# Half of each tile's gathered rows turned by VectorE in 32 by 32 blocks, and the place matmul on 128 rows

## The chip, the cores and the metric

The kernel runs on one core of one Trainium2 chip. The metric is the device time of one execution in microseconds (us). Each time of the kernel before is a median over three executions, or one profiled execution where that is said.

## The reference

448 tokens (64 sequences of 7 patches) go through three layers, one after the other. A patch of 16 by 64 values is layer-normed, multiplied by a 1024 x 512 matrix and layer-normed again. A feed-forward layer with ternary weights and 8-bit activations (1408 wide, SwiGLU) is added. Then a mixture of 32 experts with 8 chosen per token is added. The change lies in that last layer, so this is the part to keep in mind:

```
logits = x @ router_w.T ; probs = softmax(logits)
rw, sel = top_k(probs, 8) ; rw = rw / sum(rw)
for each expert e of 32:
    w_e = sum(where(sel == e, rw, 0))
    h = silu(x @ wg) * (x @ wu)          # 512 -> 192, twice
    acc = acc + (h @ wd) * w_e           # 192 -> 512
```

All of this is float32. An expert is chosen by 112 tokens on average (448 x 8 / 32), by some more, by some less.

## The kernel before

The kernel is written by hand, engine by engine, with semaphores. The first third of the program computes the two dense layers and the router. What follows is a loop over 32 **tiles**. Tile t holds the first 128 tokens that chose expert t. Tokens of an expert beyond 128 are dealt with after the loop, in lists of 32 rows, four lists to a `Quad`. That part is a loop over pairs of Quads behind the tile loop.

The routing leaves `place`, a table of 32 experts by 448 tokens: the rank of a token among those that chose the expert, or a large number. A tile t passes through these steps:

- **Place.** TensorE multiplies a one-hot column of `ident16`, broadcast to 128 columns, with `place` (`place_row`, L1145). That copies row t of the table to all 128 partitions of PSUM bank 7. The matmul contracts over 32 rows.
- **Find.** VectorE compares the row with each partition's own number and sums the matching token's index (`find`, L1623 and L1626). `idx` says which token partition p takes.
- **Gather.** GpSimd issues an indirect DMA (`gather`, L632) that fetches row `idx[p]` of the token rows from DRAM, 512 values and 32 gates. Each tile has one of eight buffers `got`, and is gathered four tiles ahead (`LEAD = 4`).
- **Turn.** TensorE transposes the 128 x 512 rows in four pieces of 128 x 128 (`transpose_x`, L1182) into PSUM; piece c takes every fourth column from c on. ScalarE copies the four pieces to `x_t` (`x_turned`, L864). `x_t` has two buffers.
- **Gate and up.** Four float32 matmuls, each of 384 columns, one for each piece (`gate_up`, L1161). The trace shows each float32 matmul as two instructions.
- **SiLU and weigh.** ScalarE takes SiLU of the gate half (`silu`, L869); VectorE multiplies it by the up half and by the token's gate (`weigh`, L1637). The result is `hid`.
- **Turn back.** TensorE transposes `hid` in two pieces (`transpose_h`, L1215 and L1218); VectorE copies them to `h_t` (`turn_back`, L1642).
- **Down.** Two tiles at a time: TensorE multiplies 128 rows and then the other 64 rows of both (`down_two`, L1190 and L1193). ScalarE copies the result (`y_out`, L875), and GpSimd adds it to the sums in DRAM with an indirect DMA (`scatter`, L646).

The order on each engine is the order of the code; nothing is rescheduled. On TensorE, iteration t is: turn t+1, gate and up of t, turn back of t-1 (if t is even), place of t+4, and if t is even, down of t-2 and t-1 and turn back of t. So the work repeats every two tiles, which is called a **pair** below. An odd tile's iteration is short, an even tile's is long. On VectorE, iteration t is: turn back of t-1 (t even), weigh t, find t+4, some work on lists at t = 3, 4 and 8, turn back of t (t even), and `keep`, which copies the index for the scatter (L1632).

Two waits matter here. Bank 7 is one buffer, so the place matmul of tile t+4 waits until `find` of tile t+3 has read it:

```
def place_row(m):
    pe.wait_ge(idx_ready, m.upto(-1))
```

And a gather waits for its own index (`pool.wait_ge(idx_ready, m.upto())`). GpSimd's order is gather t+4, and at each odd t also scatter t-3 and scatter t-2. The experts' weights are loaded by the SP queue up to 12 tiles ahead, each into its own one of 12 slots. At t = 4 and t = 8 TensorE also computes small tables for the lists and, after the down matmuls, waits for VectorE to have read them (`table_read`, `table_ready`).

## Time and profile before

| | |
|---|---|
| median of 3 executions | 307.24 us (306.87 to 307.67) |
| the profiled execution | 305.28 us, with a span of 303.5 us |
| TensorE matmuls busy | 284.3 us (94%) |
| VectorE busy | 150.9 us (50%) |
| ScalarE busy | 125.1 us (41%) |
| GpSimd busy | 126.1 us (42%) |
| mean granted TensorE clock | 0.979 of full |
| DMA | 85.53 MB, mean 282 GB/s |

The span is the time from the first to the last instruction in the profile; 1.8 us of the execution lie outside it. "Busy" is the time in which an engine works on some instruction, waits left out. Overlapping instructions of one engine count once, and the trace models where a matmul ends, so a fully busy TensorE can still have gaps between the starts of its instructions. The tile loop lies between 108 us and 274 us of the span.

### The profile page before, as it was taken

How to read it: one execution, taken by the hardware profiler on the slowest of the kernel's cores; microseconds unless marked ns; L12 is line 12 of the kernel's file. 1: busy time of each engine (PE TensorE's matmuls, PEld its weight loads, DVE VectorE, ACT ScalarE, POOL GpSimd, SP SyncE). 2: the span in 40 equal slices, each digit the busy share in tenths (PEclk: the TensorE clock that was granted, in tenths of full speed). 3: DMA queues.
4: the chain of work that ended last, by engine and by line, in shares of the span. 5: the costliest groups of instructions: out<-in, count | busy, mean ns of one | idle time of the engine just before them, and what ended most of it. 6: DMA issues, size and time to landing. Idle time of an engine off the chain costs nothing.

```text
span 303.5 us, 3905 instructions
## 1 busy us (share of the span) xinstructions
PE 284.3 (94%) x1159; PEld 145.9 (48%) x1159; DVE 150.9 (50%) x446; ACT 125.1 (41%) x213; POOL 126.1 (42%) x129
## 2 busy tenths in 40 slices
PE   4899999779999999999999999999999999998992
PEld 1345444445557355544545555465545455553231
DVE  2648999996988623243244322323332243313465
ACT  2348998999974321321321332132223213312101
POOL 3162212976520322164356336535633653455220
PEclk9999999999998599999999999999999999999998
DMA  7999999503998189699999999999999999996784
GB/s 244 344 417 425 381 405 337 173 0 134 322 324 281 42 285 313 204 270 322 316 304 349 306 312 341 337 323 312 349 324 319 313 350 304 296 298 89 139 236 133
DMA packets 27799, 85.53 MB, mean 282 GB/s; under 512 B 4209, under 2 KB 4337, under 8 KB 26785
## 3 DMA queue, kind: packets, MB, share of 16 engines
q1 hardware_dynamic: 19760, 64.78, 60.8%
q0 software_dynamic: 7488, 18.42, 26.0%
q10 hardware_dynamic: 530, 2.08, 2.5%
q8 instruction: 10, 0.16, 0.2%
q14 instruction: 11, 0.09, 0.1%
HBM read 72.34 MB, written 12.92 MB: 281 GB/s over the span
## 4 chain that ended last, share of the span: by engine, by line
PE 57%; DVE 17%; DMA 6%; issue 5%; ACT 3%; POOL 2%; POOLq 0%; DVEq 0%; ACTq 0%
PE ps L1161 25%; PE ps L1190 9%; PE ps L1182 6%; PE ps L1193 5%; DMA ring<-sum 3%; PE ps L1145 3%; DVE big L1441 2%; DVE stats L1325 2%; PE ps L1215 2%; PE ps L1048 2%; DMA sum<-w_t,add_idx 2%; PE ps L927 2%; DVE raw L1447 2%; DMA scrap<-token_rows,idx 1%; PE ps L1218 1%
## 5 line engine op out<-in xcount | busy, mean ns | idle before, releaser
L632 POOL DMA_INDIRECT scrap<-token_rows,idx x36 | 35.9, 998 | 92.2 <-DVE add_idx L1632 59.0
L646 POOL DMA_INDIRECT sum<-w_t,add_idx x32 | 51.3, 1604 | 18.6 <-issue 7.0
L864 ACT ACTIVATE w_t<-ps 128x512 f32<-128x512 f32 x36 | 21.4, 597 | 84.2 <-PE ps L1182 79.5
L1642 DVE COPY w_t<-ps 128x256 f32<-128x256 f32 x34 | 14.4, 424 | 62.0 <-PE ps L1218 50.6
L1637 DVE SCALAR_TENSOR_TENSOR w_t<-ps,scrap,w_t 128x192 f32<-128x192 f32 x32 | 13.2, 413 | 54.6 <-issue 44.5
L869 ACT ACTIVATE w_t<-ps 128x192 f32<-128x192 f32 x34 | 11.3, 331 | 55.9 <-PE ps L1161 46.8
L1161 PE MATMUL ps<-ring,w_t 128*128 128x384 f32 x96 | 33.1, 487 | 0.7 <-issue 0.7
L555 POOL TENSOR_TENSOR root_out<-root_in,minus_half 112x1 f32<-112x1 f32 x20 | 13.1, 657 | 45.7 <-DVE root_in L1342 45.6
L1161 PE MATMUL ps<-big,w_t 128*128 128x384 f32 x88 | 30.3, 487 | 0.0
L952 PE MATMUL ps<-raw,last 128*112 128x512 f32 x64 | 30.2, 624 | 0.0
L1182 PE MATMUL ps<-ident,scrap 128*128 128x128 f32 x144 | 24.9, 297 | 3.0 <-DVE h L1736 2.0
L1182 PEld LDWEIGHTS ps<-ident,scrap 128*128 128x128 f32 x144 | 20.2, 208 | 7.6 <-issue 6.0
L1161 PEld LDWEIGHTS ps<-ring,w_t 128*128 128x128 f32 x96 | 17.4, 192 | 10.4 <-issue 0.9
L1623 DVE SCALAR_TENSOR_TENSOR hit<-ps,iota_p,token 128x448 f16<-128x448 f32 x32 | 21.6, 675 | 0.9 <-PE ps L1251 0.9
L1010 PE MATMUL ps<-w_t,scrap 128*112 128x512 bf16 (+1 forms) x96 | 20.5, 363 | 1.7 <-DVE raw L1447 1.2
L1161 PEld LDWEIGHTS ps<-big,w_t 128*128 128x128 f32 x88 | 16.0, 191 | 8.7
L952 PEld LDWEIGHTS ps<-raw,last 128*112 128x112 f32 x64 | 11.5, 187 | 17.7 <-issue 17.7
L875 ACT ACTIVATE w_t<-ps 128x512 f32<-128x512 f32 x31 | 16.8, 597 | 5.1 <-PE ps L1193 5.1
L566 POOL TENSOR_TENSOR big<-raw,scrap 112x704 f32<-112x704 f32 (+1 forms) x7 | 12.7, 1828 | 8.7 <-DVE raw L1447 8.7
L1010 PEld LDWEIGHTS ps<-w_t,scrap 128*112 128x112 bf16 x96 | 11.9, 130 | 8.5 <-DVE raw L1447 1.4
L1161 PE MATMUL ps<-raw,w_t 128*128 128x384 f32 x40 | 13.7, 486 | 0.0
L711 ACT ACTIVATE scrap<-big 128x1536 bf16<-128x1536 f32 (+1 forms) x8 | 11.0, 1379 | 6.0 <-DMA big<-in_mlp_w_in 5.6
(213 smaller groups left out, 469.6 us busy)
## 6 DMA issues: line engine op xcount, KB each, us to landing
big<-in_ffn_gate_up SPq DMA_DIRECT2D x15, 768.0 KB
ring<-in_ffn_gate_up SPq DMA_DIRECT2D x13, 768.0 KB
raw<-in_ffn_gate_up SPq DMA_DIRECT2D x6, 768.0 KB
last<-in_ffn_gate_up SPq DMA_DIRECT2D x6, 768.0 KB
big<-in_ffn_w_down SPq DMA_DIRECT2D x15, 256.0 KB, 4.6
ring<-in_ffn_w_down SPq DMA_DIRECT2D x13, 256.0 KB, 4.7
big<-in_mlp_w_in SPq DMA_DIRECT2D x2, 1536.0 KB, 17.8
big<-in_mlp_w_in SPq DMA_DIRECT2D x2, 1280.0 KB, 20.4
```

What stands on the lines that cost most here:

```text
L632: nc.gpsimd.indirect_dma_start(got[:, got_at(s), :], None, rows_dram[:, :], bass.IndirectOffsetOnAxis(ap=idx[:, s:s + 1], axis=0)).then_in ...
L646: nc.gpsimd.indirect_dma_start(acc_dram[m.two][:, :], bass.IndirectOffsetOnAxis(ap=add_idx[:, m.eight:m.eight + 1], axis=0), y[:, m.four, ...
L864: nc.scalar.activation(x_t[:, m.two, :, :], bank(2 + m.two).rearrange("p (c t) -> p c t", c=4), ACT.Copy).then_inc(xt_ready, 1)
L875: nc.scalar.activation(y[:, m.four, :], bank(4 + m.two), ACT.Copy).then_inc(y_ready, 1)
L952: last = nc.tensor.matmul(acc, patch_t[g % 2][:, c, :], wtok_raw[:, c, :], start=False, stop=c == KC - 1)
L1010: last = nc.tensor.matmul(bank(3 * half_, 3)[0:G, a:a + w], q1_t[:, c, g * G:(g + 1) * G], w_t4[:, c, half_ * I1 + a:half_ * I1 + a + w], ...
L1161: last = nc.tensor.matmul(dst, x_t[:, m.two, c, :], wg[:, :, c, :], start=c == 0, stop=c == 3)
L1182: last = nc.tensor.transpose(bank(2 + m.two)[:, c * P:(c + 1) * P], got[:, got_at(m.eight), c:D:4], ident[:, :])
L1190: nc.tensor.matmul(bank(4 + m.two), h_t[:, m.two, 0, :], down_of(m.slot), start=True, stop=False)
L1193: nc.tensor.matmul(bank(4 + m.two), h_t[rows_, m.two, 1, :], down_rest_of(m.slot), start=False, stop=True).then_inc(y_done, 1)
L1623: nc.vector.scalar_tensor_tensor(hit[:, :], bank(b)[:, 0:TOK], mine, token[:, :], ALU.is_equal, ALU.mult, accum_out=idx_f[:, s:s + 1]).the ...
L1642: nc.vector.tensor_copy(h_t[:, m.two, :, :], bank(6)[:, 0:2 * P].rearrange("p (c t) -> p c t", c=2)).then_inc(ht_ready, 1)
```

## The change

It has three parts.

1. `place` now has 128 rows. GpSimd clears all of them once before the routing ends, ScalarE writes the first 32 as before, and the place matmul contracts over 128 rows. The rows that are added hold zeros. (The places of the lists still contract over 32 rows.)
2. For tiles 2 to 31 TensorE turns only pieces 0 and 1 (`pieces`). Pieces 2 and 3 are turned by VectorE in `turn_half`, straight from the gathered rows in SBUF to `x_t`: 16 instructions a tile, each transposing a block of 32 rows by 2 x 32 values. Their place in VectorE's order is after weigh of tile t, for tile t+2, ahead of find of tile t+4. `gate_up` waits for both.
3. `turn_back`, the copy of the turned gated values, moves from VectorE to ScalarE. At an even t it stands behind SiLU of t (for tile t-1), at an odd t at the head of the iteration (for tile t-1).

```
@@ -157,7 +157,7 @@
-        place = after(TOK // 2).bitcast(F16)[0:NE, :]
+        place = after(TOK // 2).bitcast(F16)
@@ -280,6 +280,10 @@
+        def pieces(m):
+
+            return 2 if isinstance(m, Tile) and m.t >= 2 else 4
+
@@ -619,6 +624,7 @@
             root(1 + NG)
+            nc.gpsimd.memset(place[:, :], 0.0).then_inc(consts, 1)
 
@@ -856,17 +862,24 @@
             act.wait_ge(rank_done, 1)
-            nc.scalar.activation(place[:, :], bank(0)[0:NE, 0:TOK], ACT.Copy).then_inc(place_ready, 1)
+            act.wait_ge(consts, 12)
+            nc.scalar.activation(place[0:NE, :], bank(0)[0:NE, 0:TOK], ACT.Copy).then_inc(place_ready, 1)
...
             def x_turned(m):
                 act.wait_ge(xt_done, m.upto())
-                nc.scalar.activation(x_t[:, m.two, :, :], bank(2 + m.two).rearrange("p (c t) -> p c t", c=4), ACT.Copy
+                n = pieces(m)
+                nc.scalar.activation(x_t[:, m.two, 0:n, :], bank(2 + m.two)[:, 0:n * P].rearrange("p (c t) -> p c t", c=n), ACT.Copy
                                      ).then_inc(xt_ready, 1)
...
+            def turn_back(m):
+                act.wait_ge(ht_done, m.upto())
+                nc.scalar.activation(h_t[:, m.two, :, :], bank(6)[:, 0:2 * P].rearrange("p (c t) -> p c t", c=2), ACT.Copy
+                                     ).then_inc(ht_ready, 1)
@@ -881,6 +894,8 @@
             for t in range(NE):
                 m = Tile(t)
+                if t % 2:
+                    turn_back(Tile(t - 1))
                 if t and t + 1 < NE:
                     x_turned(Tile(t + 1))
...
                 silu(m)
+                if t and t % 2 == 0:
+                    turn_back(Tile(t - 1))
...
@@ -1142,18 +1161,19 @@
             def place_row(m):
 
                 pe.wait_ge(idx_ready, m.upto(-1))
-                nc.tensor.matmul(bank(7)[:, 0:TOK], ident16[0:NE, m.t:m.t + 1].broadcast_to([NE, 128]), place[:, :],
+                nc.tensor.matmul(bank(7)[:, 0:TOK], ident16[:, m.t:m.t + 1].broadcast_to([128, 128]), place[:, :],
                                  start=True, stop=True).then_inc(place_done, 1)
...
             def gate_up(m):
                 wg = gate_up_of(m.slot)
                 pe.wait_ge(xt_ready, m.upto())
+                wait(pe, half_turned, m.t - 1)
...
@@ -1178,7 +1198,7 @@
-                for c in range(4):
+                for c in range(pieces(m)):
                     last = nc.tensor.transpose(bank(2 + m.two)[:, c * P:(c + 1) * P], got[:, got_at(m.eight), c:D:4], ident[:, :])
@@ -1637,10 +1657,14 @@
-            def turn_back(m):
-                dve.wait_ge(ht_done, m.upto())
-                nc.vector.tensor_copy(h_t[:, m.two, :, :], bank(6)[:, 0:2 * P].rearrange("p (c t) -> p c t", c=2)
-                                      ).then_inc(ht_ready, 1)
+            def turn_half(m):
+                dve.wait_ge(ld_got[m.eight], m.gathered())
+                for b in range(0, P, 32):
+                    for a in range(0, P, 32):
+                        last = nc.vector.transpose(
+                            x_t[b:b + 32, m.two, 2:4, a:a + 32],
+                            got[a:a + 32, got_at(m.eight), 4 * b:4 * b + 128].rearrange("p (d c) -> p c d", c=4)[:, 2:4, :])
+                last.then_inc(half_turned, 1)
@@ -1686,10 +1710,10 @@
-                if t and t % 2 == 0:
-                    turn_back(Tile(t - 1))
                 dve.wait_ge(ld_got[m.eight], m.gathered())
                 weigh(m, got[:, got_at(m.eight), D + t:D + t + 1])
+                if t + 2 < NE:
+                    turn_half(Tile(t + 2))
                 if t + LEAD < NE:
                     find(Tile(t + LEAD))
...
-                if t % 2 == 0:
-                    turn_back(m)
                 keep(m)
```

The rest of the diff renames nothing and changes only the corresponding lines of the lists and of the first four places.

TensorE's order over one pair, from the place of an odd tile's iteration on, before (names: `w_t` on the left of a place is the table, `scrap` is the buffer of gathered rows, `ident` the identity):

```order
L1145 MATMUL ps<-w_t,ident 128x448
L1182 MATMUL ps<-ident,scrap 128x128 x4
L1161 MATMUL ps<-ring,w_t 128x384 x4
L1215 MATMUL ps<-ident,w_t 128x128
L1218 MATMUL ps<-ident,w_t 128x128
L1145 MATMUL ps<-w_t,ident 128x448
L1190 MATMUL ps<-ring,w_t 128x512 x2
L1193 MATMUL ps<-ring,w_t 128x512 x2
L1215 MATMUL ps<-ident,w_t 128x128
L1218 MATMUL ps<-ident,w_t 128x128
L1182 MATMUL ps<-ident,scrap 128x128 x4
L1161 MATMUL ps<-raw,w_t 128x384 x4
```

and after the change:

```order
L1164 MATMUL ps<-w_t,ident 128x448
L1202 MATMUL ps<-ident,scrap 128x128 x2
L1181 MATMUL ps<-ring,w_t 128x384 x4
L1235 MATMUL ps<-ident,w_t 128x128
L1238 MATMUL ps<-ident,w_t 128x128
L1164 MATMUL ps<-w_t,ident 128x448
L1210 MATMUL ps<-ring,w_t 128x512 x2
L1213 MATMUL ps<-ring,w_t 128x512 x2
L1235 MATMUL ps<-ident,w_t 128x128
L1238 MATMUL ps<-ident,w_t 128x128
L1202 MATMUL ps<-ident,scrap 128x128 x2
L1181 MATMUL ps<-raw,w_t 128x384 x4
```

The turn has two transposes in the place of four; nothing else moved, and the line numbers are those of each program.

VectorE's order over an even tile's iteration before (`w_t` holds `hid`, `h_t` and `x_t`, `scrap` the gathered rows):

```order
L1642 COPY w_t<-ps 128x256
L1637 SCALAR_TENSOR_TENSOR w_t<-ps,scrap,w_t 128x192
L1623 SCALAR_TENSOR_TENSOR hit,idx_f<-ps,iota_p,token 128x448
L1626 TENSOR_SCALAR idx<-idx_f,iota_p 128x1
L1642 COPY w_t<-ps 128x256
L1632 COPY add_idx<-idx 128x1
```

and one iteration after the change, the same for odd and even tiles:

```order
L1657 SCALAR_TENSOR_TENSOR w_t<-ps,scrap,w_t 128x192
L1664 STREAM_TRANSPOSE w_t<-scrap 32x2x32 x16
L1643 SCALAR_TENSOR_TENSOR hit,idx_f<-ps,iota_p,token 128x448
L1646 TENSOR_SCALAR idx<-idx_f,iota_p 128x1
L1652 COPY add_idx<-idx 128x1
```

The two copies of the turned gated values are gone, and 16 block transposes stand between weigh and find.

## Rows read from the trace of the kernel before

**Rows 1.** The page, busy time by engine and PE clock in 40 slices

```profile
PE 284.3 (94%) x1159; PEld 145.9 (48%) x1159; DVE 150.9 (50%) x446; ACT 125.1 (41%) x213; POOL 126.1 (42%) x129
...
PEclk9999999999998599999999999999999999999998
```

**Rows 2.** By stretch: us, PE, PEld, DVE, ACT, POOL busy, PEclk, DMA share, GB/s

```profile
177.16:187.63 10.47, 10.47 (x40) 5.46 (x39) 3.34 (x13) 2.83 (x6) 5.23 (x5) 1.00 1.06 330
96.00:101.00 5.00, 4.19 (x21) 2.62 (x21) 2.98 (x20) 3.05 (x12) 0.00 (x0) 0.50 0.26 95
```

**Rows 3.** Timeline of TensorE over one pair (start us, us, then the instruction)

```profile
176.52 0.64 PE L1182 MATMUL ps<-ident,scrap 128*128 128x128 f32 x4
177.00 2.75 PE L1161 MATMUL ps<-big,w_t 128*128 128x384 f32 x8
179.68 0.36 PE L1145 MATMUL ps<-w_t,ident 32*128 32x448 f16 x1
179.97 0.75 PE L1182 MATMUL ps<-ident,scrap 128*128 128x128 f32 x4
180.55 2.75 PE L1161 MATMUL ps<-big,w_t 128*128 128x384 f32 x8
183.14 0.27 PE L1215 MATMUL ps<-ident,w_t 128*128 128x128 f32 x1
183.25 0.27 PE L1218 MATMUL ps<-ident,w_t 128*128 128x128 f32 x1
183.45 0.36 PE L1145 MATMUL ps<-w_t,ident 32*128 32x448 f16 x1
183.74 1.13 PE L1190 MATMUL ps<-ring,w_t 128*128 128x512 f32 x2
...
187.47 0.49 PE L1161 MATMUL ps<-big,w_t 128*128 128x384 f32 x1
```

**Rows 4.** Timeline of VectorE over the same pair

```profile
180.20 0.42 DVE L1637 SCALAR_TENSOR_TENSOR w_t<-ps,scrap,w_t 128x192 f32<-128x192 f32 x1 [3.00 <-issue]
180.54 0.68 DVE L1623 SCALAR_TENSOR_TENSOR hit<-ps,iota_p,token 128x448 f16<-128x448 f32 x1
...
181.26 0.21 DVE L1626 TENSOR_SCALAR idx<-idx_f,iota_p 128x1 int32<-128x1 f32 x1
...
183.56 0.43 DVE L1642 COPY w_t<-ps 128x256 f32<-128x256 f32 x1 [2.03 <-PE ps L1218]
183.90 0.41 DVE L1637 SCALAR_TENSOR_TENSOR w_t<-ps,scrap,w_t 128x192 f32<-128x192 f32 x1
```

**Rows 5.** Timeline of ScalarE, the odd tile's SiLU

```profile
179.78 0.33 ACT L869 ACTIVATE w_t<-ps 128x192 f32<-128x192 f32 x1 [1.01 <-PE ps L1161]
```

**Rows 6.** Timeline of TensorE, 448-column fillers just before the first tile

```profile
105.89 1.47 PE L927 MATMUL ps<-ranked,ident 112*128 112x448 bf16 x6
```

**Rows 7.** VectorE's small instructions: groups by form, then their timeline

```profile
L1642 DVE COPY w_t<-ps 128x256 f32<-128x256 f32 x34 | 14.4, 424 | 62.0 <-PE ps L1218 50.6 <-issue 9.4 <-PE ps L1221 2.0
L1680 DVE TENSOR_SCALAR sought<-ps,iota_p 32x24 f32<-32x24 f32 x4 | 0.9, 237 | 0.0
L1622 DVE COPY owns<-ps 128x32 f32<-128x32 f32 x4 | 0.7, 183 | 2.2 <-PE ps L1152 2.2
...
153.09 0.99 DVE L1680 TENSOR_SCALAR sought<-ps,iota_p 32x24 f32<-32x24 f32 x4
...
264.32 0.18 DVE L1622 COPY owns<-ps 128x32 f32<-128x32 f32 x1
264.42 0.67 DVE L1623 SCALAR_TENSOR_TENSOR hit<-ps,sought,token 128x448 f16<-128x448 f32 x1
```

**Rows 8.** Timeline of GpSimd, two gathers

```profile
176.98 1.02 POOL L632 DMA_INDIRECT scrap<-token_rows,idx  x1 [0.31 <-issue]
182.33 0.98 POOL L632 DMA_INDIRECT scrap<-token_rows,idx  x1 [4.32 <-DVE add_idx L1632]
```

**Rows 9.** Chain of waits, the last gather of a full list

```profile
270.21 4.30 DMA scrap<-token_rows,idx
```

More of the change, by code:

```diff
@@ L401, in program @@
         xt_ready = sem("xt_ready")
+        half_turned = sem("half_turned")
         silu_ready = sem("silu_ready")
@@ L894, in _ @@
                 x_turned(Quad(0, i))
+            turn_back(Tile(NE - 1))
             y_out(Tile(NE - 2))
@@ L900, in _ @@
                     silu(m)
+                    turn_back(m)
                 act.wait_ge(fin_ready, 4 * k + 3)
@@ L1151, in place_lists @@
                 nc.tensor.matmul(bank(7)[:, TOK:TOK + NE], pick[:, m.i, :], ident_h[0:NE, 0:NE], start=True, stop=True)
-                nc.tensor.matmul(bank(7)[:, 0:TOK], pick[:, m.i, :], place[:, :], start=True, stop=True).then_inc(place_done, 1)
+                nc.tensor.matmul(bank(7)[:, 0:TOK], pick[:, m.i, :], place[0:NE, :], start=True, stop=True).then_inc(place_done, 1)
             def gate_up(m):
@@ L1250, in _ @@
             for t, b in ((0, 7), (1, 4), (2, 5), (3, 6)):
-                nc.tensor.matmul(bank(b)[:, 0:TOK], ident16[0:NE, t:t + 1].broadcast_to([NE, 128]), place[:, :],
+                nc.tensor.matmul(bank(b)[:, 0:TOK], ident16[:, t:t + 1].broadcast_to([128, 128]), place[:, :],
                                  start=True, stop=True).then_inc(place_done, 1)
@@ L1706, in _ @@
                     dve.sem_inc(h_ready, 4)
-                if t % 2 == 0:
-                    turn_back(m)
                 keep(m)
-            turn_back(Tile(NE - 1))
             m = Tile(NE - 1)
@@ L1729, in _ @@
                     weigh(m, gate_w[:, m.i:m.i + 1])
-                    turn_back(m)
                 for i in range(2):
```

## The prediction

> **What bounds the kernel now.** The page comes first: TensorE is busy 94% of the span, the others 50% or less, and its clock is granted nearly in full [rows 1]. A 94% is an average, so the tile loop is read by itself. The busy times of one pair of tiles show 10.47 us of TensorE in 10.47 us [rows 2], and each pair in the middle of the loop has the same length. VectorE is busy for 3.34 us of it, GpSimd for 5.23. TensorE therefore sets the pace, and what counts is the distance between the starts of its instructions. The timeline of one pair gives them [rows 3]: turn of a tile 0.48 (176.52 to 177.00), gate and up 2.58 to 2.68, place 0.29, turn 0.58, gate and up 2.59, and so on to the next pair at 187.47. From here on time zero is 177.00, the start of the odd tile's gate and up, and "at 6.45" means 183.45 in the rows.
>
> Three more things are read for what the change will lengthen. VectorE's timeline [rows 4]: weigh of the odd tile starts at 3.20, find of the tile four further on at 3.54, and its last instruction ends at 4.47 (181.26 + 0.21). TensorE wants that index at 6.45, for the place matmul of the even iteration, since bank 7 must be free. So today there are 2 us to spare. The same VectorE starts the even tile's weigh at 6.90.
>
> **Part 1, place on 128 rows.** Around each place matmul TensorE loses time. Ahead of the one at 179.68, gate and up takes 2.68, against 2.59 ahead of a 128-row instruction (180.55 to 183.14). Place then keeps 0.29, where fillers of 112 rows and as many columns kept at most 0.22 ((1.47 - 0.36) / 5, with the clock rising within them) [rows 3, 6]; at the full clock I take 0.19. The turn behind it takes 0.58 instead of 0.48. That is 0.10 + 0.10 + 0.10 = 0.30 for each place, 0.60 a pair. Clearing the table is one GpSimd instruction before the routing ends, where GpSimd waits: nothing.
>
> **Part 2, half of the turn.** TensorE saves two of four transposes, 0.24 a tile, 0.48 a pair. The pair would then take 10.47 - 0.60 - 0.48 = 9.39 us if nothing waited. ScalarE copies 256 columns instead of 512, which helps it.
>
> VectorE gets 16 block transposes a tile, for 30 tiles. None is in this trace, so their price d is bounded. By form, a copy of 32 values takes 183 ns and one of 256 values 424 [rows 7], so 64 values come to 183 + 32 x 1.08 = 217 ns. Whether the next one may start before that ends decides. A 32-value copy on all 128 partitions is followed after 0.10 us (264.32 to 264.42) [rows 7]; 64 values would then be followed after 0.134. But the four L1680 instructions, each on another group of 32 partitions, span 0.99, so they start 0.25 apart with a length of 0.237 each: they don't overlap at all [rows 7]. The block transposes read another group of 32 partitions each time, as L1680 does. I take d = 0.217 + 0.015 = 0.232, so 3.7 us a tile; the ends are 0.134 and 0.27.
>
> The Trainium skill, "VectorE: DVE Perf Modes", section "Two Vector instructions with no wait between them", has a rule for this: an instruction whose inputs or output start in another quadrant than the last ones is held until all earlier ones have finished. L1680 agrees. The same page's errata section prices an SBUF instruction at 58 + 64 cycles of 0.96 GHz, 0.127 us; with that estimate the sum would be that of the first rival below.
>
> Now the path. Find of tile t+4 is queued behind the 16. Its index comes at 4.47 + 3.7 = 8.2 instead of 4.47, and TensorE sees it some 0.09 later (SiLU ends at 180.11, weigh starts at 180.20 [rows 5, 4]). TensorE arrives at that place matmul at 6.45 - 0.30 - 0.24 - 0.09 = 5.82, and waits 2.45 us, with about 0.1 to restart. **The pair takes 9.39 + 2.45 + 0.1 = 11.94 us, 1.47 more than today.** In general it is 8.2 + 16d. The odd iteration's place doesn't wait: its index was found a tile earlier. Such waits fall in the iterations t = 2, 4, ... 28: 14 of them, 20.6 us.
>
> VectorE is itself late: it is free for the even tile's weigh only at 4.47 + 3.7 + 0.13 = 8.3, and done with the next find at 8.3 + 0.34 + 3.7 + 0.93 = 13.3. In most pairs nobody needs this before 14. At t = 4 and t = 8, though, TensorE waits at 11.4 for VectorE to have read the tables, some 0.35 and 1.2 behind that find: 2.2 and 3.1 us, together 5.
>
> **Part 3, turn back on ScalarE.** VectorE loses two copies of 0.34 a pair, which stood where it was idle. ScalarE does SiLU of the even tile, then the copy: about 1.3 after gate and up's last instruction, when the second down matmul's weights are just wanted. Nothing, or 0.1.
>
> **Ends.** Tiles 0 and 1 wait for nothing new: -0.3. After the loop the chain runs over the last lists' index, two scatters and the last gather (4.30 us) [rows 9]; find is 3.7 later, of which 1.5 is in the pair already: +2.2.
>
> **Sum:** 20.6 + 5 - 0.3 + 2.2 = +27.5 us. On the profiled execution (305.28 us) this gives 332.8; the median shown is 2 us above that execution, and I forecast against it: 307.24 + 27.5, say 334.5 us.
>
> **Rivals.**
>
> *The block transposes overlap* (d = 0.134). For: other small copies do [rows 7]. Against: L1680. 16d is 2.1, the wait 0.9 + 0.1, the pair 10.4, 14 x -0.1 = -1.4; the tables cost 2.2, the tail 2.2: +2.7, so 310 us.
>
> *The change is faster than before*: one mechanism, VectorE moving two values a cycle and overlapping as well. L1680 and the f32 rate of 1.08 ns a value speak against it. 64 values would then stream in the time of 32, so d = 0.10 (264.32 to 264.42), the index comes at 6.1, the wait is 0.35 + 0.1, the pair 9.84, and 14 x -0.63 = -8.8 with +2.3 at the ends gives 301 us. It decides below d = 0.12: there the pair's gain covers tables and tail.
>
> *The gather becomes the bound.* VectorE's 16 transposes wait for rows whose gather was issued behind the find before. That circle is 0.86 from index to issue (181.47 to 182.33) [rows 4, 8], the latency, 16d and 0.93 of find: 5.5 us + latency. The latency is over the 4.30 of the idle end [rows 9], and under 8.1: the gather of 182.33 was in time for a turn at 190.4, a pair after 179.97. Over 6.4 us it would be longer than the path above; at 8.1 the pair takes 13.6 and the kernel 358 us. Against it: a slower loop asks less of the DMA.
>
> *The clock falls.* TensorE idles a fifth of each pair, and it was granted half its clock from 96 to 101 us, behind busy stretches with gaps [rows 2, 1]. It would double some 5.8 us of each pair: over 400 us. The few-hundred-ns gaps of the loop never did it.
>
> *Part 1 doesn't save what it should.* The wait would hide 0.2 of the 0.3 before it: +0.2 a pair, 337 us, within my range.
>
> **Chances.** Forecast with no overlap 0.62, overlap 0.18, faster mechanism 0.10, gather 0.07, clock 0.03. Faster by over 0.3% (about what a measurement of this kernel tells from no change): 0.10 and a part of the overlap, 0.13. Same 0.05. Slower 0.82. The range reaches from the overlapping case, 309, to d = 0.27 (12.5 us a pair, +38), 345; it leaves out the fast case, the clock and most of the gather's.
>
> **What would show it.** L1664 at 0.22 to 0.25 us apart; TensorE idle for 2 to 2.5 us ahead of the even iteration's place (L1164), released by `idx` (L1646), and 11.9 us a pair; TensorE's turn at 0.24, and 2.6 rather than 2.68 ahead of place. Transposes 0.14 apart, or a pair under 10.5, would prove me wrong. A wait on the gather ahead of L1664 would speak for the third rival.

## The result, and the profile after

| | before | after |
|---|---|---|
| median | 307.46 us (306.87 to 309.34, 4 executions) | 370.12 us (369.28 to 370.59, 4 executions) |
| the profiled execution, its span | 305.28 us, 303.5 us | 370.21 us, 368.4 us |

The ratio is 1.206, 95% interval 1.200 to 1.212. The change costs 63 us, where 27 were forecast, and 370 us lies outside the forecast's range. In some of the experiments below a few executions ran in a slower state: the medians are over all executions, the ratios over the others alone.

The page after, the same lines as [rows 1]:

```profile
PE 300.3 (82%) x1099; PEld 148.5 (40%) x1099; DVE 272.3 (74%) x892; ACT 128.3 (35%) x247; POOL 126.6 (34%) x130
...
PEclk9999999999769896896969889689887898789998
```

TensorE is busy 82% of the span, no longer 94%. Its busy time has grown all the same, by 16 us, with 60 instructions fewer: its clock is granted only in part all through the tile loop, where before it was full. VectorE has gone from 50% to 74%.

TensorE's timeline of one pair, to be laid beside [rows 3] (start us, us, instruction; in brackets the idle time before it and what ended it):

```profile
251.71 2.75 PE L1181 MATMUL ps<-raw,w_t 128*128 128x384 f32 x8
254.30 0.35 PE L1164 MATMUL ps<-w_t,ident 128*128 128x448 f16 x1
254.49 0.39 PE L1202 MATMUL ps<-ident,scrap 128*128 128x128 f32 x2
254.71 2.75 PE L1181 MATMUL ps<-raw,w_t 128*128 128x384 f32 x8
...
257.40 0.27 PE L1238 MATMUL ps<-ident,w_t 128*128 128x128 f32 x1
260.98 0.56 PE L1164 MATMUL ps<-w_t,ident 128*128 128x448 f16 x1 [3.31 <-DVE idx L1646]
261.33 1.91 PE L1210 MATMUL ps<-ring,w_t 128*128 128x512 f32 x2
263.04 1.44 PE L1210 MATMUL ps<-raw,w_t 128*128 128x512 f32 x2
...
265.98 0.81 PE L1181 MATMUL ps<-big,w_t 128*128 128x384 f32 x2
```

The first four rows are as forecast: gate and up 2.59 ahead of the 128-row place, place 0.19, turn 0.22. Then comes the forecast wait, at the forecast place and on the forecast releaser, but 3.31 us long. And behind it there is something that was not forecast: the first two instructions of the down matmuls span 1.71 us (261.33 to 263.04), twice the 0.86 that they take at the full clock (a run below shows it). The pair takes 14.27 us.

VectorE's timeline of the same pair, against [rows 4]:

```profile
254.92 0.42 DVE L1657 SCALAR_TENSOR_TENSOR w_t<-ps,scrap,w_t 128x192 f32<-128x192 f32 x1 [2.45 <-issue]
255.25 4.70 DVE L1664 STREAM_TRANSPOSE w_t<-scrap 32x64 f32<-32x64 f32 x16
259.98 0.68 DVE L1643 SCALAR_TENSOR_TENSOR hit<-ps,iota_p,token 128x448 f16<-128x448 f32 x1
...
260.71 0.21 DVE L1646 TENSOR_SCALAR idx<-idx_f,iota_p 128x1 int32<-128x1 f32 x1
```

and the group of the transposes (busy us, mean ns | idle before them and what ended it):

```profile
L1664 DVE STREAM_TRANSPOSE w_t<-scrap 32x64 f32<-32x64 f32 x480 | 135.0, 281 | 6.8 <-DMA scrap<-token_rows,idx 0.7
```

Find stands 4.73 us behind the first transpose, so one takes 0.295 from start to start with a length of 0.281. They don't overlap. The index is there at 260.92, which is 9.21 on the prediction's clock (its time zero is 251.71).

Where the clock goes, in the same stretch (us, busy times, PEclk, DMA share, GB/s):

```profile
250.28:260.50 10.22, 7.39 (x29) 4.14 (x29) 7.43 (x26) 2.96 (x8) 2.62 (x2) 1.00 0.96 243
260.50:263.93 3.43, 2.95 (x5) 1.36 (x5) 3.27 (x15) 0.00 (x0) 1.84 (x2) 0.51 0.68 217
263.93:274.15 10.22, 8.02 (x31) 4.28 (x29) 7.66 (x28) 2.96 (x8) 3.39 (x3) 1.00 0.89 242
274.15:280.98 6.83, 5.73 (x9) 1.88 (x9) 5.87 (x23) 0.00 (x0) 4.21 (x3) 0.50 0.80 200
280.98:291.22 10.24, 6.93 (x29) 4.34 (x28) 7.10 (x27) 2.96 (x8) 1.02 (x1) 1.00 0.97 265
```

The clock is full (2.4 GHz) for 10.2 us, then at half (1.2 GHz) for 3.4 or 6.8 us, and so on through the loop: fourteen times between 124 and 325 us. Each fall lies between 1.1 us before the end of a long wait of TensorE and 0.4 us behind it, so the half stretch lies over the down matmuls.

Last, the waits (us in total, times, longest) that bear on the place matmul:

```profile
PEld ps L1164 <- DVE idx L1646: 48.3, 14, 3.5
...
PE ps L1164 <- DVE idx L1646: 44.7, 14, 3.3
```

Thirteen of the fourteen are at even iterations' places, as forecast, and one is at the odd place of the first pair, which was not. The fourteenth even one, at t = 28, stands at the place of the lists (L1170, 3.31 us).

**The sum after.** From the start of tile 1's gate and up to tile 29's there are 14 pairs: 147.7 us before, 212.8 after (113.31 to 326.13), 65.1 more. The forecast's arithmetic, 8.2 + 16d, with the measured d of 0.295 gives 12.92 a pair. The trace lets each pair be cut in two at the even iteration's place. From the second pair on that place starts 9.26 to 9.28 us after the pair's start, every time. What stands behind it takes 3.59 us at the full clock (a run below shows it), and here 5.0, 5.2, 6.4 or, in the pairs with the tables, 7.1 and 7.7 us. A pair at the full clock is then 9.27 + 3.59 = 12.86, 2.39 over the 10.47 of before, or 33.5 us for 14. In the first pair TensorE waits at both places, 2.36 and 2.59 us, and the even place comes 1.8 us later than in the others. The second and the fourth pair, which hold the tables, take 0.8 and 1.3 us more than other pairs with as long a half stretch: 2.1. What is left behind the places is 28.8 us, between 1.4 and 2.9 a pair. The pairs before had held 1.1 us over 14 x 10.47, so 33.5 + 1.8 + 2.1 + 28.8 - 1.1 = 65.1. Outside the 14 pairs the span is the same within 0.2 us. So two things have to be tested: that a transpose on another group of partitions costs 0.295, and that the 28.8 us behind the places are the clock's and that it falls for the wait.

### The profile page after: what moved, and what is told of

Read it like the earlier page. It is cut to its first block and busy times, and to the rows that moved or that the text cites. A ratio compares the mean times of both kernels' runs of the same rounds, so it can differ in the third digit from the quotient of the medians.

```text
span 368.4 us, 4299 instructions
## 1 busy us (share of the span) xinstructions
PE 300.3 (82%) x1099; PEld 148.5 (40%) x1099; DVE 272.3 (74%) x892; ACT 128.3 (35%) x247; POOL 126.6 (34%) x130
## 3 DMA queue, kind: packets, MB, share of 16 engines
HBM read 72.34 MB, written 12.92 MB: 231 GB/s over the span
## 5 line engine op out<-in xcount | busy, mean ns | idle before, releaser
L1664 DVE STREAM_TRANSPOSE w_t<-scrap 32x64 f32<-32x64 f32 x480 | 135.0, 281 | 6.8 <-DMA scrap<-token_rows,idx 0.7
L881 ACT ACTIVATE w_t<-ps 128x256 f32<-128x256 f32 x34 | 13.0, 381 | 127.2 <-PE ps L1238 124.0
L1164 PE MATMUL ps<-w_t,ident 128*128 128x448 f16 x28 | 11.9, 426 | 44.7 <-DVE idx L1646 44.7
L1181 PE MATMUL ps<-ring,w_t 128*128 128x384 f32 x96 | 33.1, 487 | 0.7 <-issue 0.7
L1164 PEld LDWEIGHTS ps<-w_t,ident 128*128 128x128 bf16 x28 | 2.8, 100 | 50.2 <-DVE idx L1646 48.3
L872 ACT ACTIVATE w_t<-ps 128x256 f32<-128x256 f32 (+1 forms) x36 | 14.9, 417 | 20.3 <-PE ps L1202 19.1
L1210 PE MATMUL ps<-big,w_t 128*128 128x512 f32 x22 | 19.4, 1009 | 0.0
L1210 PE MATMUL ps<-ring,w_t 128*128 128x512 f32 x24 | 19.3, 925 | 0.0
L888 ACT ACTIVATE w_t<-ps 128x512 f32<-128x512 f32 x31 | 17.0, 609 | 2.3 <-PE ps L1213 2.3
L1202 PE MATMUL ps<-ident,scrap 128*128 128x128 f32 x84 | 15.9, 284 | 2.1 <-DVE h L1756 1.8
```

What stands on the lines that cost most here:

```text
L872: nc.scalar.activation(x_t[:, m.two, 0:n, :], bank(2 + m.two)[:, 0:n * P].rearrange("p (c t) -> p c t", c=n), ACT.Copy).then_inc(xt_ready, 1)
L888: nc.scalar.activation(y[:, m.four, :], bank(4 + m.two), ACT.Copy).then_inc(y_ready, 1)
L1164: nc.tensor.matmul(bank(7)[:, 0:TOK], ident16[:, m.t:m.t + 1].broadcast_to([128, 128]), place[:, :], start=True, stop=True).then_inc(place ...
L1181: last = nc.tensor.matmul(dst, x_t[:, m.two, c, :], wg[:, :, c, :], start=c == 0, stop=c == 3)
L1202: last = nc.tensor.transpose(bank(2 + m.two)[:, c * P:(c + 1) * P], got[:, got_at(m.eight), c:D:4], ident[:, :])
L1210: nc.tensor.matmul(bank(4 + m.two), h_t[:, m.two, 0, :], down_of(m.slot), start=True, stop=False)
```

## The experiments

Each kernel was run beside the kernel before on the same chip; the ratios are to that (its medians in the three sets are 306.86, 307.51 and 306.44 us). Diffs are against the changed kernel unless said otherwise. "Pair" is again the distance from one odd tile's gate and up to the next.

### Part 1 alone

```
# against the kernel before
-        place = after(TOK // 2).bitcast(F16)[0:NE, :]
+        place = after(TOK // 2).bitcast(F16)
-... ident16[0:NE, m.t:m.t + 1].broadcast_to([NE, 128]), place[:, :],
+... ident16[:, m.t:m.t + 1].broadcast_to([128, 128]), place[:, :],
```

> The kernel before with part 1 alone (place on 128 rows), nothing else changed. Theory: each place matmul then costs 0.30 us less of TensorE's time, a pair 9.87 us in place of 10.47, the clock stays granted in full, and the kernel takes about 8 to 9 us less than before, some 299 us. Rival 1: the fall of the clock in the changed kernel comes from the 128-row place and not from the waits; then slices with half the clock show up here too and the time goes up. Rival 2: the gathers or the weights can't keep up with a shorter pair; then TensorE waits on DMA and less than half of the 8 us is seen.

Measured: 305.80 us (10 executions), ratio 0.996 (0.993 to 1.000). TensorE's timeline of a pair:

```profile
173.34 2.75 PE L1163 MATMUL ps<-big,w_t 128*128 128x384 f32 x8
175.92 0.35 PE L1147 MATMUL ps<-w_t,ident 128*128 128x448 f16 x1
176.11 0.67 PE L1184 MATMUL ps<-ident,scrap 128*128 128x128 f32 x4
176.62 2.75 PE L1163 MATMUL ps<-big,w_t 128*128 128x384 f32 x8
...
183.23 0.49 PE L1163 MATMUL ps<-big,w_t 128*128 128x384 f32 x1
```

Gate and up 2.58, place 0.19, turn 0.51: 3.28 where it was 3.55 [rows 3]. Undisturbed pairs take 9.86 against 10.47: 0.61, the forecast's 0.60. The 14 pairs take 142.0 us against 147.7. Of these 5.7 us the whole keeps 1.1 (305.80 against 306.86 for the kernel before in this set). The waits of this kernel show where the rest went:

```profile
POOL scrap L633 <- DMA sum<-w_t,add_idx: 15.1, 4, 3.9
...
POOL sum L647 <- DMA sum<-w_t,add_idx: 9.8, 4, 4.6
...
PEld ps L1184 <- DMA scrap<-token_rows,idx: 8.1, 10, 3.9
```

The scatters into the sums finish late, behind them the gathers of the lists start late, and from tile 31 on the kernel needs 39.9 us where the kernel before needs 33.2. The clock is at half from 269.5 to 276.3 us as well. TensorE's saving becomes waiting for DMA at the end. The forecast of 299 us is missed, and the second rival holds: less than half of the 8 us is seen. The first doesn't: with the 128-row place the clock is full through the loop up to 269.5 us.

### Parts 1 and 3, no VectorE turn

```
             def pieces(m):
-            return 2 if isinstance(m, Tile) and m.t >= 2 else 4
+            return 4
-                if t + 2 < NE:
-                    turn_half(Tile(t + 2))
```

> The changed kernel without part 2: TensorE turns all four pieces again, the turn back stays on ScalarE, place on 128 rows. Theory: moving the turn back costs nothing, so the time is that of part 1 alone within 0.5 us (about 299 us). Rival: the copy on ScalarE comes too late for the second down matmul of a pair, 0.1 to 0.5 us a pair, so 1.5 to 7 us more than part 1 alone.

Measured: 304.04 us (4 executions), ratio 0.988 (0.983 to 0.994), pairs of 9.86 as with part 1 alone. No cost of part 3 can be seen, as forecast; the time forecast with it, 299 us, is missed like that of part 1. The same kernel a second time, with ten executions:

> Parts 1 and 3 without part 2, a second time, beside the runs above on the same chip. Expected: 304 us again (303 to 306), 0.985 to 0.995 of the kernel before.

Measured: 306.07 us, ratio 0.9963 (0.9931 to 0.9995). That is just above the 303 to 306 expected, and the intervals of the two just touch. No version measured is clearly better than this one, and its own gain is small: 0.4% here, 1.2% in the first measurement.

### Four wide transposes

Sixteen transposes of 32 rows become four of 128 rows. One instruction transposes the four 32-row groups each within itself.

```
-                    for a in range(0, P, 32):
-                        last = nc.vector.transpose(
-                            x_t[b:b + 32, m.two, 2:4, a:a + 32],
-                            got[a:a + 32, got_at(m.eight), 4 * b:4 * b + 128]...)
+                    last = nc.vector.transpose(
+                        x_t[:, m.two, 2:4, b:b + 32],
+                        got[:, got_at(m.eight), 4 * b:4 * b + 128]...)
```

> The changed kernel with 4 transposes on all 128 partitions in place of the 16 on 32; each block stays in its own group of 32 partitions, so pieces 2 and 3 are not the transposed rows and the products are wrong, but as much data moves. Theory: the cost is one of instructions, not of data: about 0.2 us each, 0.8 us a tile, the index comes in time (5.3 against 5.8), a pair takes 9.4 us, the clock is full, and the kernel takes about 291 to 294 us. Rival: the cost is one of data through the transposing part; then VectorE still spends over 3 us a tile and the pair stays over 11 us.

Measured: 310.61 us, ratio 1.0065 (1.0012 to 1.0118). Two rows, from the timeline and from the waits:

```profile
209.87 0.84 DVE L1663 STREAM_TRANSPOSE w_t<-scrap 128x64 f32<-128x64 f32 x4 [2.58 <-DMA scrap<-token_rows,idx]
```

```profile
DVE w_t L1663 <- DMA scrap<-token_rows,idx: 34.2, 15, 4.1
...
PEld ps L1202 <- DMA scrap<-token_rows,idx: 14.5, 14, 3.6
```

The forecast of 291 to 294 us is missed by 17 us, although its theory holds: the cost is one of instructions, not of data. The four take about 0.8 us and start 0.17 to 0.21 apart with lengths of 0.25 to 0.29: here they do overlap, and TensorE waits for no index from L1646. Two pairs out of 14 take 9.38 and 9.37 us, the 9.39 that the forecast gave for a pair in which nothing waits. The others are 9.9 to 14.5, because now the rows themselves come too late; the longest, 14.5, is a pair with tables, where VectorE waited 4.1 us for rows and TensorE then 3.8 us for VectorE. This is the forecast's third rival, the gather: it decides as soon as the loop is fast enough to need it.

### Sixteen transposes that stay in their group of rows

```
-                            got[a:a + 32, got_at(m.eight), 4 * b:4 * b + 128]...
+                            got[b:b + 32, got_at(m.eight), 4 * a:4 * a + 128]...
```

> The changed kernel with the same 16 transposes of 32 rows, but each reads and writes the same group of 32 partitions, and four in a row stay in one group (the products are wrong for pieces 2 and 3). Theory: an instruction that changes the group starts only after the one before has ended, one that doesn't may overlap it: 12 of 16 then stand about 0.17 us apart and 4 stand 0.295 apart, 3.2 us a tile in place of 4.7, the index comes 1.5 us earlier and a pair takes about 11.4 us if the clock holds. Rival: block transposes never overlap; then they stay 0.295 apart and the time is that of the changed kernel (370 us).

Measured: 337.94 us, ratio 1.100 (1.092 to 1.107). VectorE's timeline:

```profile
211.63 3.28 DVE L1664 STREAM_TRANSPOSE w_t<-scrap 32x64 f32<-32x64 f32 x16
214.94 0.68 DVE L1643 SCALAR_TENSOR_TENSOR hit<-ps,iota_p,token 128x448 f16<-128x448 f32 x1
```

The same 16 instructions on as many values take 3.3 us instead of 4.7. Read one by one, they start 0.17 to 0.22 apart where input and output stay in the group of the one before, and 0.254 apart where both change to the next group. The lengths of all 480 in the changed kernel and of all 480 here (ns: shortest, median, longest):

```profile
L1664 DVE STREAM_TRANSPOSE w_t<-scrap x480: 266/282/299, 112.7 to 334.1; 32x64 f32<-32x64 f32 x160
```

```profile
L1664 DVE STREAM_TRANSPOSE w_t<-scrap x480: 233/243/297, 112.2 to 300.9; 32x64 f32<-32x64 f32 x160
```

It is tempting to put the longer ones down to the way from one group to another. The traces say otherwise. In the changed kernel 4 of each 16 (a = b) stay in their own group too, and they take 0.27 to 0.29 like their neighbours. In this run all stay in their own group, and the first in each new group still takes 0.28, as here at 212.45, against the 0.24 of one that follows in the same group, at 212.84:

```profile
212.45 0.28 DVE L1664 STREAM_TRANSPOSE w_t<-scrap 32x64 f32<-32x64 f32 x1
212.84 0.24 DVE L1664 STREAM_TRANSPOSE w_t<-scrap 32x64 f32<-32x64 f32 x1
```

So the wait for the end of the one before, and not the way between groups, makes 0.295 out of 0.175. An instruction that has to start behind the end of the one before it takes 0.28, and the next, if the group changes again, stands 0.014 behind its end. One that may start while the one before still runs takes 0.24 and is followed after 0.175. The Trainium skill, "VectorE: DVE Perf Modes", section "Two Vector instructions with no wait between them", has the hold itself (an instruction whose input or output starts in another quadrant than the last one's is held until the earlier ones have finished); the trace agrees, 0.254 against 0.175. The same page's errata section would have it at 0.127 us (58 + 64 cycles of 0.96 GHz); the lengths measured here, 0.24 and 0.28, are about twice that.

TensorE still waits here for the index, 21 times for 1.9 us at most. Two pairs take the 11.4 us that were expected; the later ones take 12.0 to 12.7, since VectorE waits 12 times, 31.4 us in all, for gathered rows ahead of its transposes. The clock is full through the middle of the loop:

```profile
185.00:300.00 115.00, 93.57 (x325) 47.72 (x324) 84.22 (x395) 29.14 (x78) 49.86 (x39) 1.00 0.97 285
```

### Half the transposes

```
-                    for a in range(0, P, 32):
+                    for a in range(0, P, 64):
```

> The changed kernel with 8 of the 16 block transposes left out (every second group of input rows, so the products are wrong). Theory: the wait is the number of transposes times 0.295 us, the index comes at 6.9 in place of 9.2, TensorE waits 1.1 us a pair, the clock mostly holds, a pair takes 10.6 us where the gathers keep up and up to 11 where not: 312 to 320 us. Rival: the blocks' cost isn't on the path and the clock alone made the loss; then the time stays over 340 us or the clock still falls in every pair.

Measured: 324.51 us, ratio 1.056 (1.045 to 1.067), above the 312 to 320 expected. Pairs of 10.5 to 11.9 us behind the tables. By the forecast's formula eight transposes give 8.2 + 8 x 0.295 = 10.56, which the quickest pairs show (10.49, 10.51). The longer ones wait for rows, too: VectorE waits 40.8 us in all for gathers ahead of L1664. Between the first tile and the last the clock is at half for two stretches of 3.4 us only, at the two waits for the tables (3.5 and 4.0 us). So halving the transposes takes away three quarters of the loss (17.0 us are left of 63), and not half.

### The transposes behind find

```
                 weigh(m, ...)
-                if t + 2 < NE:
-                    turn_half(Tile(t + 2))
                 if t + LEAD < NE:
                     find(Tile(t + LEAD))
+                if t + 2 < NE:
+                    turn_half(Tile(t + 2))
```

> The changed kernel with the 16 transposes behind find of the same iteration, not ahead of it. Theory: the wait for the index goes, but VectorE itself is then the bound: 2 x (4.72 + 0.34 + 0.93 + 0.13) = 12.2 us a pair, the weigh coming late for the turn back; 330 to 336 us if the clock holds, up to 350 if TensorE's idle time still lowers it. Rival: only the place in the order mattered and VectorE's late weigh is hidden; then a pair takes under 11 us and the kernel under 315 us.

Measured: 338.52 us, ratio 1.101 (1.092 to 1.111). The pair, and the loop's middle:

```profile
240.24:252.25 12.01, 9.67 (x35) 5.17 (x34) 11.46 (x43) 2.95 (x9) 5.22 (x4) 1.00 1.02 311
185.00:300.00 115.00, 94.42 (x322) 50.21 (x321) 109.76 (x405) 27.80 (x75) 51.06 (x39) 0.97 1.01 284
```

A pair takes 12.01 us and VectorE never rests: weigh, find and 16 transposes are 6.0 us a tile. The order on VectorE, with what it does to the clock, costs 32 us of the 63, but no order makes this change pay, since 12.0 is over the 10.47 of the kernel before. TensorE now idles in two pieces, 0.5 and 1.9 us, and the clock falls in two pairs of those between 185 and 300 us.

### Part 1 undone

```
# the four lines of part 1 back to those of the kernel before
```

> The changed kernel with part 1 undone (place on 32 rows again). Theory: what part 1 saves ahead of the wait is hidden by the wait, so a pair is 0.1 to 0.3 us longer and the kernel takes 1 to 5 us more than the changed one, 371 to 375 us, with the clock falling in the same way. Rival: the 128-row place takes part in the fall of the clock; then the clock falls less often here and the time is lower by 5 us or more.

Measured: 375.68 us, ratio 1.222 (1.206 to 1.239), 5.6 above the changed kernel and just over the range expected; the two intervals overlap, so the pairs of the profiled executions have to speak. The wait is shorter by what TensorE comes later, 3.00 us in place of 3.31, so the saving at the odd iteration's place is hidden; that at the even one lies behind the wait and counts: at the full clock 3.78 us from the even place to the pair's end, in place of 3.59. The 14 pairs take 216.6 us, 3.8 more than in the changed kernel, 0.27 each.

```profile
262.72 0.36 PE L1162 MATMUL ps<-w_t,ident 32*128 32x448 f16 x1 [3.00 <-DVE idx L1644]
```

From 206 us on pairs alternate between 14.7 and 16.0, with the clock at half once in each. Before that the waits that end at 168.7 and 202.9 us, of 2.99 and 3.00, pass without a fall, and a pair takes 13.05 at 193.65. The clock falls 12 times in place of 14, but the time is not lower, so nothing here speaks for the rival.

### The wait filled with work

TensorE gets 18 matmuls of 112 rows by 448 columns, results unused, ahead of the even iteration's place, so that it doesn't idle while it waits.

```
             def place_row(m):
+                if m.t % 2 == 0 and m.t >= 6:
+                    keep_busy(18, 2)
                 pe.wait_ge(idx_ready, m.upto(-1))
```

> The changed kernel, with 18 filler matmuls (448 columns, 16 bit, about 0.19 us each at full clock) on TensorE ahead of each even iteration's place matmul, where it waits for the index now; nothing else waits longer for them. Theory: the clock falls because TensorE stands idle for 3.4 us in each pair, so with fillers the slices at half clock go, a pair takes 12.9 to 13.0 us in place of 15.2, and the kernel 340 us, some 30 less. Rival: the clock falls for what VectorE does, or for TensorE's mean load; then it falls here too and the time stays at 365 us or more.

Measured: 365.97 us, ratio 1.191 (1.181 to 1.200). The forecast time of 340 us is missed by 26, and the time alone would have spoken for the rival. It is 4 us less than the changed kernel, although TensorE does more, but the two intervals just touch. The trace decides. The fillers of one pair:

```profile
269.10 3.57 PE L946 MATMUL ps<-ranked,ident 112*128 112x448 bf16 x18
```

From 183 to 316 us the clock is full, with VectorE's work and the order unchanged. Up to the last tile it falls four times in place of fourteen, at 118.2, 145.5, 176.3 and 316.2 us, and by each fall lies a wait that the fillers don't cover: 2.37 us in the first pair, 2.92 and 4.20 for the tables, and 2.61 near the end. The pairs at the full clock are 12.88 to 14.63 us. The one at 262.55, and the waits of VectorE in this kernel:

```profile
262.55:276.08 13.53, 12.95 (x54) 6.78 (x53) 11.18 (x41) 2.95 (x9) 5.21 (x5) 1.00 0.90 254
```

```profile
DVE w_t L1666 <- DMA scrap<-token_rows,idx: 16.7, 10, 2.5
```

One of them, in VectorE's timeline, and what GpSimd issued before:

```profile
274.02 2.98 DVE L1666 STREAM_TRANSPOSE w_t<-scrap 32x64 f32<-32x64 f32 x10 [1.83 <-DMA scrap<-token_rows,idx]
```

```profile
260.41 1.62 POOL L652 DMA_INDIRECT sum<-w_t,add_idx  x1 [0.30 <-issue]
262.34 1.60 POOL L652 DMA_INDIRECT sum<-w_t,add_idx  x1 [0.30 <-issue]
266.67 1.02 POOL L638 DMA_INDIRECT scrap<-token_rows,idx  x1 [2.73 <-DVE w_t L1659]
```

The rows for the transposes at 274.02 are those of the gather issued at 266.67: 7.4 us, where the idle end of the kernel before had 4.30 [rows 9]. Two scatters stand before it on GpSimd's queue (the DMA engines are also 0.90 busy in this pair; which of the two delays it, this run alone does not show). With the clock mended, the gather takes its place.

### The same, with the scatters behind the next gather

```
-                if t % 2 and t >= 3:
-                    scatter(Tile(t - 3))
-                    scatter(Tile(t - 2))
+                if t % 2 == 0 and t >= 4:
+                    scatter(Tile(t - 4))
+                    scatter(Tile(t - 3))
```

> The changed kernel with the 18 fillers, and on GpSimd the two scatters moved from each odd iteration to behind the gather of the next even one. In the run with fillers alone the clock was granted in full from 183 us to 316 us, but a pair took 13 to 14.6 us. Theory: there VectorE's transposes waited for the even tile's gather, whose data was queued behind the two scatters' for 6 to 7 us; with the scatters behind it the gather lands in about 3 us, the wait for it goes, and a pair takes 12.9 to 13.1 us where the clock is full; 345 to 350 us. Rival: something else than the gather made the pairs longer than 12.94; then they stay at 13.5 us or more and the time at 360 us or more.

Measured: 367.09 us, ratio 1.198 (1.188 to 1.208), where 345 to 350 were expected. As a way to a faster kernel it failed; the pairs tell why, and settle the question of the clock. Three of them:

```profile
247.74:260.62 12.88, 12.88 (x55) 6.70 (x54) 10.00 (x37) 2.96 (x9) 5.18 (x4) 1.00 0.94 259
194.55:207.43 12.88, 12.88 (x55) 6.78 (x53) 10.67 (x39) 2.95 (x9) 5.18 (x4) 1.00 0.92 268
275.15:288.02 12.87, 12.87 (x55) 6.79 (x54) 10.96 (x41) 2.96 (x9) 5.19 (x4) 1.00 0.90 259
```

Five of the nine pairs between 194 and 316 us take 12.86 to 12.88 us: the forecast's 8.2 + 16d with the measured d, and no more. In them the place comes 9.29 us after the pair's start (257.03 from 247.74), as in the changed kernel (9.27), and what is behind it takes 3.59 instead of 5.00. So those 1.4 us are the clock's, and so is what the other pairs of the changed kernel need beyond 3.59 behind the same place, tables aside: 28.8 us in all. The down matmuls at the full clock:

```profile
257.03 0.36 PE L1168 MATMUL ps<-w_t,ident 128*128 128x448 f16 x1
257.23 1.02 PE L1214 MATMUL ps<-ring,w_t 128*128 128x512 f32 x2
258.09 1.02 PE L1214 MATMUL ps<-raw,w_t 128*128 128x512 f32 x2
```

The other four take 0.8 to 1.9 us more. VectorE's waits for rows ahead of its transposes fall from 16.7 to 6.4 us in all, 1.8 at most, and in the last of the four the clock is at half for 3.4 us. But the end, from tile 31 on, takes 38.1 us where it was 33.1, with waits for the late scatters in it:

```profile
ACT scrap L894 <- DMA sum<-w_t,add_idx: 5.6, 1, 5.6
...
DVE w_t L1739 <- DMA sum<-w_t,add_idx: 5.0, 1, 5.0
```

### The late scatters without the VectorE turn

The same move of the scatters in the version with parts 1 and 3, and in the kernel before.

> Parts 1 and 3 alone, with the same move of the scatters. Theory: in the run of parts 1 and 3 TensorE waited 16 us for gathers, because a shorter pair leaves them less time behind the scatters; with the scatters later the gathers land in time, most pairs take 9.86 us, and the time is 298 to 301 us. Rival: the DMA engines are the bound by their bandwidth; then the scatters only push the wait elsewhere and the time stays at 303 to 306 us.

> The kernel before, with the same move of the scatters alone. Theory: its pairs are bound by TensorE at 10.47 us and no wait for a gather lies on the path but the last one; the last gather is issued ahead of two scatters, which brings 1 to 3 us, so 304 to 306 us against 307. Rival: the scatters at the end of the loop then finish later and cost as much, so no difference.

Measured: 307.20 us, ratio 1.0027 (0.9993 to 1.0061), and 311.96 us, ratio 1.0082 (1.0027 to 1.0137). Both miss their gain; the second is slower than the kernel before. The ten executions of the first spread from 302.53 to 309.52 us. (The 16 us in its expectation add the waits of weight loads, 10.6, to those of matmuls, 5.6, which are in part the same time.) Waits for the sums are still there in both (7.2, 4.6 and 3.8 us in the first; 7.2, 5.6, 5.3 and 4.4 in the second), on GpSimd and ScalarE. What orders those transfers at the end was not taken apart.

## Why the prediction was wrong

**What bounds the kernel, the place of the wait and its releaser: right.** TensorE had set the pace before; in the changed kernel there are 14 waits ahead of the even iteration's place, released by `idx`, and none ahead of the odd one's but in the first pair.

**Part 1: right.** 0.61 us a pair measured alone, 0.60 forecast (of the kernel's time alone it gave 1.1 us). **Part 3: right**, nothing. The turn at half length: 0.22 to 0.24 us a tile, as forecast.

**"I take d = 0.217 + 0.015 = 0.232": the first step that failed.** It was right that nothing overlaps, and that decided against the overlapping rival and the faster one. The length was mis-sized: 0.281 and not 0.217, so d is 0.295, above the upper end of 0.27. The spacing was read from L1680, whose instructions are held, but the length from copies, of which the short one (264.32) starts 0.09 us before the end of the instruction ahead of it. The run with the transposes inside their groups shows what that does: the same instruction takes 0.24 when it overlaps and 0.28 when it is held. The forecast had the better row in hand. L1680 has 24 values in 0.237; with 40 more at the forecast's 1.08 ns that is 0.280, and d is 0.295. That this fits so well may be luck, since L1680 is another instruction; that it stands above the copies' 0.217 is what should have widened the range. 16 x 0.063 is 1.0 us a pair, 14 us in all. The formula held: 8.2 + 16 x 0.295 = 12.92, and pairs of 12.86 to 12.88 came once the clock was full.

**"The few-hundred-ns gaps of the loop never did it": the second step, and the larger.** The clock rival had a chance of 0.03 and a price of 5.8 us a pair, some 80 in all. It came true at 1.4 to 2.9 us a pair, 29 us. Two errors stand in that paragraph. The evidence against it was of gaps of a few hundred ns, while the forecast itself put a gap of 2.45 us into every pair; the evidence did not bear on what was to come. And "it would double some 5.8 us of each pair" took the clock as either full or at half for good. It alternates: 10.2 us at full, 3.4 or 6.8 at half. A rival with the mechanism right and its price three times too high looked like one that could be left out.

The two errors hang together. With the wait at 3.31 the clock falls in every pair, at 3.00 (part 1 undone) in 11 of 13. With waits up to 1.9 us, or the idle time cut in two, it fell seldom, and with work in the wait it stayed full for 130 us. The first pairs have a few waits of the forecast's size: by one of 2.37 and one of 2.35 us (the two kernels with fillers) the clock fell, and also with 2.36 and 2.59 in one pair (the changed kernel), but not with 2.06 and 2.40 (part 1 undone). So it could have fallen at the forecast's 2.45; whether in every pair no run shows.

**Tables, 5 us: not what happened.** The forecast had waits of 2.2 and 3.1 us for them. Measured are 0.45 and 0.95 us, since the down matmuls ahead of them ran at half the clock and came late themselves; the two pairs cost 0.8 and 1.3 us more than others, and the kernel before had held 1.1 there. With the clock full, in the kernel with fillers, the waits are 2.92 and 4.20. The first pair's wait at the odd place, 1.8 us, was not in the forecast. **Ends, -0.3 and +2.2**: +0.3 and -0.4. The later find did not lengthen the end. The gather in the chain takes 3.40 us there, where it had 4.30 [rows 9]; the rest of that difference was not followed.

```profile
336.45 3.40 DMA scrap<-token_rows,idx
```

**The gather: right as a rival, and next in line.** It does not bind the changed kernel, because that is slow. VectorE waits for rows for 34.2 us in all with four wide transposes, 40.8 with half of them, 31.4 with the transposes inside their groups, and 16.7 in the filled kernel.

So of the 37 us by which the span missed, 13 are the transpose's price (14 x (12.86 - 11.94); 14 by the formula's 12.92), 29 the clock's, -2 the tables' and the first pair's, and -2 the ends'. The 29 are read behind the even places of one trace, against the 3.59 us that the same instructions take in the runs with a full clock. (The forecast's own last step, 307.24 + 27.5, is 334.7 and not 334.5.)

## What to carry to other kernels

Before a small instruction is put 16 times on an engine that has time, look for what is queued behind it on that engine and who waits for that; here 4.7 us of VectorE work went straight to TensorE, although VectorE was half idle. The order alone (find ahead of the transposes) gives back half of the loss, and most of the rest is the count: 12.0 us of VectorE work in a pair that took 10.47.

When an instruction's price is put together from rows, take the length from a row that is held in the same way as the new one, and let the range reach up to the dearest such row.

When a forecast puts a new idle gap on TensorE, it has to ask what the clock does at that gap, and not at those that the old trace has; the price is read from the stretches at half, which come and go, and not by doubling everything.

## What the runs showed of the hardware

- A 32 x 64 float32 transpose on VectorE whose input or output starts in another group of 32 partitions than the last one's takes 0.28 us, and a row of them stands 0.295 apart, whether each goes to another group or stays in its own. One that follows in the same group takes 0.24 and starts 0.175 after the last. On all 128 partitions, within each group, four times the values cost no more: 0.26, and 0.17 to 0.21 apart.
- With a wait of 3.3 us in each pair of 14 to 17 us TensorE's clock went between full for 10.2 us and half for 3.4 or 6.8 us for 200 us on end. Matmuls whose results nobody needs, put into that wait, kept it full for 133 us. A pair without a wait for rows then took 12.88 us, fillers included, and not 14.3 to 15.8.
- A place matmul over 32 rows between float32 matmuls over 128 rows costs 0.3 us more than one over 128 rows (pairs of 10.47 and 9.86 us with two of them each).
- A gather behind two scatters on GpSimd's queue, with the DMA engines 0.90 busy, had its rows there 7.4 us after the start of its issue; one at the end stands in the chain with 3.4.
